# Row probabilities at the end of ACT's mixing batch, four row buffers in the expert blocks, attention products interleaved and three weight buffers, in a four-stage hybrid layer

## The reference

```python
x = x + attention(layernorm(x))      # linear attention, 8 heads, rope, elu + 1 features, plus a 3-tap convolution
x = x + experts(layernorm(x))        # softmax over 8 experts, best 2 per token, SwiGLU 256 -> 512 -> 256
x = x + mix(layernorm(x))            # time mixing, then channel mixing, see below
x = x + experts(layernorm(x))        # the same expert weights again
```

```python
# attention
q, k = split(x @ qk_w + qk_b); q = elu(q) + 1; k = elu(k) + 1
z = 1 / (q . mean_n(k) + 1e-6);  kv = rope(k)^T x / sqrt(n);  out = (rope(q) kv) * z + conv1d(x, lepe_w) + lepe_b
# experts
scores = softmax(x @ gate_w.T); top2;  y = (silu(x @ w1[e]) * (x @ w3[e])) @ w2[e];  out[token] += y * score
# mix, time part: k, v, r from mixtures of each token with the one before it
tau2 = max(eps - w, k); alpha, beta, eps = exp(eps-w-tau2)*alpha + exp(k-tau2)*v, ..., tau2   # a scan over the tokens
x = x + (out * sigmoid(r)) @ w_output
# mix, channel part
x = x + sigmoid(fr) * (square(relu(fk)) @ f_w_value)
```

## Time and profile before

| | |
|---|---|
| median of 3 runs | 1770.49 us (1768.41 to 1777.91) |
| profiled execution, its own time | 1768.61 us |
| its span in the profile | 1766.8 us |
| instructions | 28651 |
| mean granted TensorE clock | 0.873 |
| busy: PE, weight loads, DVE, ACT, POOL | 1411.7, 1187.6, 1016.4, 615.4, 785.0 us |
| DMA | 157.6 MB, mean 89 GB/s |

### The profile page before, as it was taken

The page is one execution under the profiler, slowest core; times in us unless marked ns, Lnnn a source line. Parts: engine busy times, 40 slices in busy tenths (PEclk is TensorE's granted clock), DMA queues, the critical chain, the costliest instruction groups (busy, mean ns, idle before and its releaser), DMA issues. The chain is left out here.

```text
span 1766.8 us, 28651 instructions
## 1 busy us (share of the span) xinstructions
PE 1411.7 (80%) x7528; PEld 1187.6 (67%) x7529; DVE 1016.4 (58%) x2226; ACT 615.4 (35%) x1400; POOL 785.0 (44%) x608
## 2 busy tenths in 40 slices
PE   5999974899999994378495867748774799999997
PEld 5888874688888884155364554536564578888886
DVE  5756656344444442798866868595634444444443
ACT  3555643222323332342424324233432223233332
POOL 4555633344545553443533436162323245445553
PEclk9888885899999997689697888878886799999999
DMA  6646462755543334200000000000000854643332
GB/s 203 219 157 213 156 239 100 235 122 120 137 109 56 55 54 111 85 1 12 13 12 12 12 12 12 24 0 25 13 25 24 303 146 101 153 92 54 54 54 42
DMA packets 100857, 157.63 MB, mean 89 GB/s; under 512 B 10256, under 2 KB 60688, under 8 KB 100816
## 3 DMA queue, kind: packets, MB, share of 16 engines
q1 hardware_dynamic: 73120, 118.67, 19.7%
q0 software_dynamic: 27264, 37.82, 13.0%
q10 hardware_dynamic: 432, 0.66, 0.2%
HBM read 95.89 MB, written 61.21 MB: 89 GB/s over the span
## 5 line engine op out<-in xcount | busy, mean ns | idle before, releaser
L1756 PE MATMUL bank<-b_fv,b_hT 128*128 128x256 f32 x512 | 123.6, 403 | 88.5 <-ACT b_hT L1374 88.5
L924 POOL DMA_INDIRECT x_rows<-first_y,first_add_token x71 | 112.6, 1586 | 167.5 <-DMA x_rows<-first_y,first_add_token 67.3
L924 POOL DMA_INDIRECT out_x<-second_y,second_add_token x71 | 112.5, 1585 | 166.9 <-DMA out_x<-second_y,second_add_token 59.5
L1756 PEld LDWEIGHTS bank<-b_fv,b_hT 128*128 128x128 f32 x512 | 103.7, 204 | 107.1 <-ACT b_hT L1374 91.6
L1075 DVE TENSOR_TENSOR second_hT_lo<-bank,second_hT_hi 128x512 fp32r<-128x512 f32 x71 | 49.1, 692 | 166.5 <-ACT second_hT_hi L958 157.3
L1075 DVE TENSOR_TENSOR first_hT_lo<-bank,first_hT_hi 128x512 fp32r<-128x512 f32 x71 | 49.1, 692 | 162.1 <-ACT first_hT_hi L958 152.9
L153 PE MATMUL bank<-second_ring,second_xT_hi 128*128 x284 | 120.0, 423 | 2.2 <-DVE second_xT_lo L1063 2.2
L153 PE MATMUL bank<-first_ring,first_xT_hi 128*128 x284 | 119.7, 422 | 2.2 <-DVE first_xT_lo L1063 2.2
L155 PE MATMUL bank<-second_ring,second_xT_lo 128*128 x284 | 113.1, 398 | 0.0
L154 PE MATMUL bank<-first_ring,first_xT_hi 128*128 x284 | 112.9, 397 | 0.0
L155 PE MATMUL bank<-first_ring,first_xT_lo 128*128 x284 | 112.8, 397 | 0.0
(11 more groups left out here) (354 smaller groups left out, 4193.1 us busy)
## 6 DMA issues: line engine op xcount, KB each, us to landing
first_ring<-split_weights SPq DMA_DIRECT2D x96, 256.0 KB
second_ring<-split_weights SPq DMA_DIRECT2D x96, 256.0 KB
a_wraw<-in_L_ffn_w SPq DMA_DIRECT2D x24, 512.0 KB, 4.4
split_weights<-a_whi SPq DMA_DIRECT2D x24, 512.0 KB, 2.7
split_weights<-a_wlo SPq DMA_DIRECT2D x24, 512.0 KB, 3.8
normed_rows<-xg SPq DMA_DIRECT2D x16, 528.0 KB, 3.0
x_rows<-x SPq DMA_DIRECT2D x8, 512.0 KB, 5.0
x<-x_rows SPq DMA_DIRECT2D x8, 512.0 KB, 9.3
```

The costliest lines, as they stand in the source:

```text
L924: nc.gpsimd.indirect_dma_start(x_dram[:], bass.IndirectOffsetOnAxis(ap=add_token[par][:], axis=0), y[par][:], None, compute_op=ALU.add).th ...
L1756: last = nc.tensor.matmul(out[:, j * C:(j + 1) * C], src(i, j), w[:, i, :], start=(i == 0), stop=(i == chunks - 1))
```

## The change

1. Mixing: ACT's `row_finish(b)` moves from between chunks 6 and 7 of `hidden` to the end of ACT's batch.
2. Experts: four buffers for `xs`, `y` and both token columns; gathers are issued three blocks ahead; `y` lies in tiles of the routing part; SP loads expert 1 no longer at once but together with 2 and 3; the loop body is four blocks.
3. Attention: statistics, POOL's shifts and the normalising of `xn` run a batch further ahead, and `xn` of the next batch is normalised at the start of ACT's batch; TensorE's convolution is cut into other pieces between gate, k and z products; the three weight pieces have a buffer each, and the third piece's high and low parts are made earlier in the batch; batches 5, 6 and 7 are written out.

The diff, cut to its core (renamed parameters and buffer counts that repeat are left out):

```diff
@@ over_batches
-    with engine.Fori(1, B - 2, 2) as b:
+    with engine.Fori(1, B - 4, 2) as b:
         body(b, 1)
         body(b + 1, 0)
+    body(B - 3, 1)
+    body(B - 2, 0)
     body(B - 1, 1)
@@ attention, buffers wraw, whi, wlo and their semaphores
-        wraw = [sb(f"a_wraw{i}", [P, PIECE]) for i in range(2)]
+        wraw = [sb(f"a_wraw{i}", [P, PIECE]) for i in range(3)]
+        def has_second(b):
+            return not (isinstance(b, int) and b + 2 >= B)
@@ attention, SP
-                i = (par + n) % 2
-                earlier = (3 * par + n) // 2
-                wait_count(sp, w_stored[i], 48 * (b - par) + 32 * earlier)
+                wait_count(sp, w_stored[n], 32 * b)
@@ SP's period
-                load_piece(b, par, 0)
-                load_piece(b, par, 1)
+                for n in range(3):
+                    load_piece(b, n)
                 if not is_first(b):
                     store_x(b - 1)
-                store_piece(b, par, 0)
-                load_piece(b, par, 2)
-                store_piece(b, par, 1)
+                store_piece(b, 0)
+                store_piece(b, 1)
+                store_piece(b, 2)
                 if not is_first(b):
                     store_rows(b - 1)
-                store_piece(b, par, 2)
@@ ACT's period
+                if not is_last(b):
+                    act.wait_ge(rstd_ready, b + 2)
+                    wait_count(act, kv_done, b)
+                    normalise(xn[1 - par], mv, shift, b + 1, xn_ready)
                 wait_count(act, q_ready, b)
...
                 if not is_first(b):
                     route_before(b)
-                if not is_last(b):
-                    act.wait_ge(rstd_ready, b + 2)
-                    normalise(xn[1 - par], mv, shift, b + 1, xn_ready)
-                high_part(b, par, 0)
+                high_part(b, 0)
...
                 if not is_first(b):
                     row_exp(b)
+                high_part(b, 2)
                 if not is_last(b):
                     evacuate_next(round_next(b), 1 - par)
                 if not is_first(b):
                     row_finish(b)
-                high_part(b, par, 2)
@@ POOL
             add_bias(0)
+            pool.wait_ge(var_ready, 2)
+            rstd(mv, shift, rstd_ready)
...
                 own.round(b + 1)
-                if not is_last(b):
-                    wait_apart(pool, var_ready, b + 2, passed["pool"])
-                    rstd(mv, shift, rstd_ready)
...
                     add_bias(b + 1)
+                if has_second(b):
+                    wait_apart(pool, var_ready, b + 3, passed["pool"])
+                    rstd(mv, shift, rstd_ready)
@@ DVE
             dve.wait_ge(x1_in, 16)
+            dve.wait_ge(xn_ready, 1)
+            statistics(bn, mv, 1, var_ready)
...
                 own.round(b + 1)
-                if isinstance(b, int) and b == 1 or not isinstance(b, int):
-                    dve.wait_ge(x_in, 16)
-                if not is_last(b):
-                    statistics(bn, mv, b + 1, var_ready)
...
-                weight_low(b, par, 0)
+                weight_low(b, 0)
+                if has_second(b):
+                    dve.wait_ge(x_in, 16)
+                    wait_apart(dve, xn_ready, b + 2, passed["dve"])
+                    statistics(bn, mv, b + 2, var_ready)
...
                 own.link(nc.vector.reciprocal(zr[:], zr[:]))
+                weight_low(b, 2)
...
-                weight_low(b, par, 2)
                 own.pad()
@@ TensorE
                 convolution(par, 1)
-                convolution(par, 2)
+                convolution(par, 2, (0,))
                 if not is_first(b):
                     gate_transposes(b)
-                convolution(par, 3, (0, 1))
+                convolution(par, 2, (1, 2))
                 if not is_first(b):
                     gate_products(b)
+                convolution(par, 3, (0,))
...
                 last.then_inc(z_done, 1)
+                convolution(par, 3, (1,))
@@ over_blocks
-    assert NBLK % 2 == 1
-    for i in range(3):
-        body(i, i % 2)
-    with engine.Fori(3, NBLK - 3, 2) as i:
-        body(i, 1)
-        body(i + 1, 0)
-    for i in range(NBLK - 2, NBLK):
-        body(i, i % 2)
+    assert NBLK % 4 == 3
+    for i in range(7):
+        body(i, i % 4)
+    with engine.Fori(7, NBLK - 7, 4) as i:
+        for n in range(4):
+            body(i + n, (3 + n) % 4)
+    for i in range(NBLK - 4, NBLK):
+        body(i, i % 4)
@@ experts, buffers (NX = 4 of xs, gather_token, add_token and loaded)
-        y = [sb(f"y{i}", [P, C]) for i in range(2)]
+        homes = [chosen[:].rearrange("p k e t -> p (k e t)")] + [t[:].rearrange("p k j b -> p (k j b)") for t in block_hot]
+        y = [t[:, 0:C] for t in homes]
@@ experts, SP
             load(0)
-            load(1)
             announce(0)
-            announce(1)
             sp.wait_ge(xt_done, 2)
-            for n in range(2, NS):
+            for n in range(1, NS):
                 load(n)
-            for n in range(2, NS):
+            for n in range(1, NS):
                 announce(n)
@@ experts, POOL
-                    pool.wait_ge(row_used, i - 1)
+                    pool.wait_ge(row_used, i - NX + 1)
...
             pool.wait_ge(rows_stored, 16 * B)
-            gather(0, 0)
-            gather(1, 1)
+            for i in range(NX - 1):
+                gather(i, i)
             pool.wait_ge(x_stored, 16 * B)
...
-                if not (isinstance(i, int) and i >= NBLK - 2):
-                    gather(i + 2, par)
+                if not (isinstance(i, int) and i > NBLK - NX):
+                    gather(i + NX - 1, (q + NX - 1) % NX)
                 if not is_first(i):
-                    add(i - 1, 1 - par)
+                    add(i - 1, (q - 1) % NX)
@@ experts, ACT's evacuate_y
-                if not (isinstance(i, int) and i < 2):
-                    act.wait_ge(added, 16 * (i - 1))
+                if not (isinstance(i, int) and i < NX):
+                    act.wait_ge(added, 16 * (i - NX + 1))
@@ experts, DVE
-            for i in range(2):
+            for i in range(NX):
                 nc.vector.tensor_copy(gather_token[i][:], column(row_token, i)).then_inc(token_ready, 1)
@@ mixing, ACT's hidden
-                    if not static(b, 0) and m == 6:
-                        row_finish(b)
@@ mixing, ACT's period
                 if has_next(b, 2):
                     evacuate_xn(b + 2)
+                if not static(b, 0):
+                    row_finish(b)
```

More of the change, by code:

```diff
@@ L382, in _ @@
             store_rows(B - 1)
-            sp.wait_ge(w_stored[0], 32 * (3 * B // 2))
-            sp.wait_ge(w_stored[1], 32 * (3 * B // 2))
+            for n in range(3):
+                sp.wait_ge(w_stored[n], 32 * B)
         @block.scalar
@@ L417, in row_finish, with high_part @@
                 row_probabilities(nc, df, total, xg, row_ready)
[L419 to L423, removed]
+            def high_part(b, n):
+                act.wait_ge(wraw_in[n], 16 * b + 16)
+                nc.scalar.activation(whi[n][:], wraw[n][:], ACT.Copy).then_inc(whi_ready, 1)
             def normalise(dst, mvt, shifts, b, done):
@@ L812, in phase_experts @@
         spare = sb("spare", [P, BW])
-        xs = [sb(f"xs{i}", [P, RW]) for i in range(2)]
+        xs = [sb(f"xs{i}", [P, RW]) for i in range(NX)]
         score = [sb(f"score{i}", [P, 1]) for i in range(2)]
@@ L833, in phase_experts @@
         w_ready, w_given, row_used = sem("w_ready"), sem("w_given"), sem("row_used")
-        loaded = [sem(f"loaded{i}") for i in range(2)]
+        loaded = [sem(f"loaded{i}") for i in range(NX)]
         added = sem("added")
@@ L905, in _, with gather, add @@
             nc.gpsimd.tensor_copy(expert_of[:], picked[:, :, 0]).then_inc(expert_ready, 1)
-            def gather(i, par):
-                if isinstance(i, int) and i < 2:
+            def gather(i, q):
+                if isinstance(i, int) and i < NX:
                     pool.wait_ge(token_ready, i + 1)
                 else:
-                    pool.wait_ge(row_used, i - 1)
+                    pool.wait_ge(row_used, i - NX + 1)
                 pool.sem_inc(passed["pool"], 1)
-                nc.gpsimd.indirect_dma_start(xs[par][:], None, normed_dram[:],
-                                             bass.IndirectOffsetOnAxis(ap=gather_token[par][:], axis=0)
-                                             ).then_inc(loaded[par], 16)
-            def add(i, par):
+                nc.gpsimd.indirect_dma_start(xs[q][:], None, normed_dram[:],
+                                             bass.IndirectOffsetOnAxis(ap=gather_token[q][:], axis=0)
+                                             ).then_inc(loaded[q], 16)
+            def add(i, q):
                 wait_apart(pool, y_evac, i + 1, passed["pool"])
@@ L975, in _, with step @@
             give_weights(0)
-            def step(i, par):
+            def step(i, q):
```

(19 more changed lines are left out.)

56 lines of the change are left out of this document (27 added, 29 removed).

## The result

The changed kernel takes 1668.96 us in the median of 4 runs (1664.73 to 1671.75), the kernel before 1769.93 (4 runs). The ratio is 0.9419, 95% interval 0.9389 to 0.9450. The profiled execution took 1667.1 us, 101.5 less than that of before (1768.6); the prediction had 107.1.

What follows compares the result with a forecast made beforehand. It took TensorE as nearly full in attention and experts, and mixing as held by waits for `b_total`. Terms 67.4 + 21.3 + 18.4 = 107.1 off 1768.6 gave 1661.5, plus 1.9 for the median: 1663 us, range 1636 to 1702.

Steps and rivals of the forecast that it cites:

- Part 1: Mixing: row probabilities last in ACT's batch remove the wait between chunks 6 and 7; 67.4 us off, bounds 54 to 73.
- the ring: Mixing: ACT stands for DVE's `b_total` before chunk 7 of `b_hT`, TensorE waits for ACT, and DVE idles 10.92 us.
- the 11.7 a batch: Mixing, batches 1 to 5: 12.7 us saved less a wait of up to 1 us, 58.5 us in all.
- Part 2: Attention: earlier statistics and normalising remove six waits at the gate products and keep the clock; 21.3 us off, ends 8 and 31.
- The term for the batch: Attention: a batch falls from 31.2 to 27.0 us, between 25.6 and 28.6; 6 x 4.2 = 25.2 us off.
- The start: Attention, first batch: ACT normalises batch 1 before batch 0's exponentials, so `a_kr` comes later; a cost of 5.4 us.
- Part 3: Expert stages: earlier first gathers (5.6 us) and half of the remaining waits (12.8 us); 18.4 us off.
- L146 waits near 0: Mixing: predicted sign that ACT's wait at L146, for `b_total`, nearly vanishes.
- (a): Rival: mixing gains as predicted, attention and experts a third, with a falling clock and late gathers; 1687 us, chance 0.20.
- (b): Rival: mixing's wait comes back through the low clock, then late k and sg for POOL; 1686 us, chance 0.10.
- (d): Rival: ACT meets `b_total` again before work TensorE needs, so half of mixing's gain is all; 1736 us, chance 0.03.
- (c): Rival: the four-block expert loop makes TensorE wait for instructions; slower, 1805 us at 1 us a block, chance 0.02.

Runs made afterwards that it cites:

- reciprocal-first run: The changed kernel with DVE's long reciprocal of the quotient in mixing moved ahead of the short `b_xn` passes; 1638.50 us, ratio 0.9254.

## Why the prediction was right, and where its terms were off

The time was 6 us above the forecast, well in its range. Two terms were too high by 12.1 together, one too low by 6.5.

**Part 1: 67.4 predicted, 63.3 measured.** The wait was what held the ring, as said. The term mis-sized is the 11.7 a batch: it was 10.5 in four batches and 11.2 in the fifth. DVE's wait at L1685 is 1.2 us, about as allowed, and its idle time fell by 11.5 in a batch, but its busy time rose from 58.8 to 59.8. The four `b_xn` passes went from 3.40 to 4.12, since POOL's pass over `b_fs` now stands beside them. The prediction had weighed just this and left it out, because "the reciprocal that stands beside it reads one tile". The reciprocal was indeed not slowed, but `b_xn` stands ahead of it. The Trainium skill ("SBUF — State Buffer", "Who interferes with whom") has a one-input DVE instruction outside the 2-port modes free of POOL, while a copy or `tensor_scalar` can be blocked for a whole instruction; the reciprocal-first run agrees, with 6.55 against 2.09 and 0.17. By that rule I had given 55, too low, since I priced POOL's pass at 2.43 us, a neighbour's time; it takes 1.08, and took 1.04 in the trace before. The copy was held up in that trace already:

```profile
944.07 2.07 DVE L1566 COPY b_mv_all<-b_scales 128x4 f32 x1 [0.15 <-DVE b_d L1628]
...
960.54 1.04 POOL L1527 TENSOR_SCALAR b_fs<-b_fs 128x1024 f32<-128x1024 f32 x1 [11.82 <-ACT b_fs L1385]
```

Two other steps of DVE changed as well: the step that makes `b_xfk_hi` takes 0.9 us longer in a batch and `b_dT` 0.5 less, for reasons that no run takes apart. Batch 6 gave 8.9 (8.0 predicted), batch 7 0.8 (0.9).

**Part 2: 21.3 predicted, 27.8 measured.** The term for the batch was mis-sized: 27.0 us was a choice between a clock that holds (25.6) and one that falls (28.6). It held at 1.00, and the batch was 24.96, better than the better case. Two errors in this term worked against each other. It started from one batch of 31.2 us where the six took 30.4 each, which is 4.7 us too much gain; and it ended at 27.0, which is 12.2 too little. The six gave 32.8 instead of 25.2. (The 27.0 taken for batch 7 stands in no row either; its row has 26.60.) The start was mis-sized the other way: the low clock behind the wait was left out, and together they cost 8.2. That the wait came out at the 5.4 worked out is partly luck, as it was 2.0 to 3.6 in four other traces of the same first batch. The tail's 3.2 us were not in the sum beyond the 1.5 for batch 7.

**Part 3: 18.4 predicted, 10.4 measured.** Two terms failed. The first gather was to land 2.8 us a stage earlier; its waits fell by 1.9 and 2.1. In the second stage the gather took 4.24 us, not 3.5, and the DMA engines were 0.90 busy meanwhile: expert 0's load still goes beside it. That this is the cause was not tried by a run. And the deferral was priced at nothing, without a reason given: SP's 24 further issues ahead of the announcement cost 7.7 us of wait in the second stage. The later waits for gathers fell by 4.1 and 6.9, 11.0 against 12.8; but part of the 6.9 was hidden by the new wait. These waits together make 7.3 of the 10.4 us. The other 3 are no waits; TensorE's busy time in the two stages fell by about that much, and no run shows why.

**The signs.** Mixing batches were 68 us apart (67 predicted, over 70 would have spoken against it), attention's 25 (27), the waits at the gate products gone but for the last, the gap at 36 to 41 there. "L146 waits near 0" was badly put: the wait is still 5.1 us a batch, only off the path. DVE's wait at L1685 (L1677 before) was to be under 1 us and is 1.2. A first wait for a gather under 6 us was missed by 0.3 in one stage, and the other waits fell to half in the second stage only (5.5 of 12.4; 9.1 of 13.2 in the first).

**The rivals.** Of (a) the clock did not fall, but the gathers did give a little over half of what was expected. (b) and (d) did not come. (c) neither: an undisturbed block takes 4.87 us (4.88 before).

## What to carry to other kernels

A moved wait is worth what it had hidden on the next engine, so list each engine's busy time beside its idle time before and after: here 11.5 us less idle time became 10.5 of gain. When transfers are deferred, follow the announcement through the issuing queue, not only the data. And look for short instructions with long durations: a copy of four columns that took 2.09 us pointed to 27 us. And before a gain is put down to an edit, look at the stretches that the edit doesn't touch: the first attention batch alone moved by up to 4 us between traces of the same code.

## What the runs showed of the hardware

- A DVE instruction can stand for the rest of a POOL instruction: 2.09 us for a copy of 128x4 that takes 0.17 alone, ended within 0.1 us of POOL's (the same in six batches of the kernel before). A reciprocal of 128x1024 took 6.54 to 6.55 either way.
- The granted clock moved with small changes among small products. One wait of 1.3 us in a batch, with a busy TensorE on both sides, went with a clock of 0.85 instead of 1.00 and 4.9 us a batch; without that wait but with the old pieces it was 0.89. Which pause or product decides was not tried; only that both edits are needed.
- An indirect add of 128 rows took 3.7 to 3.9 us in quiet stretches and 6.7 to 8.6 beside weight loads, with the DMA engines' busy share at 0.88 or more. That pacing the loads would save time was not tried.
